# A selective scan on one core: eight scan units in flight instead of four, C products two units at a time, sums three units later in TensorE's order

## The reference, cut to what matters

```python
proj = hidden_states @ W_in.T
u, gate = jnp.split(proj, 2, axis=-1)            # 1024 channels each
u = silu(conv1d(u) + conv_b)                      # 4 taps, depthwise
dt, Bm, Cm = jnp.split(u @ Wx.T, [32, 48], -1)    # each rms-normed, 16 states
delta = softplus(dt @ Wdt.T + dt_bias)
state = exp(delta_t * A) * state + (delta_t * u_t) * B_t     # per step t
y_t = sum over the 16 states of state * C_t
y = (y + u * D_param) * silu(gate)
return y @ W_out.T
```

## Time and profile before

| | |
|---|---|
| runs (3) | 1966.2 to 1977.37 us, median 1969.73 |
| profiled execution | 1971.7 us, span 1969.9 us |
| PE busy | 1608.2 us, 82% |
| DVE busy | 1381.4 us, 70% |
| ACT busy | 1091.1 us, 55% |
| POOL busy | 1009.7 us, 51% |
| mean granted clock of PE | 0.83 of full |

### The profile page before, as it was taken

The page is one execution under the profiler, slowest core; times in us unless marked ns, Lnnn a source line. Parts: engine busy times, 40 slices in busy tenths (PEclk is TensorE's granted clock), DMA queues, the critical chain, the costliest instruction groups (busy, mean ns, idle before and its releaser), DMA issues. The chain is left out here.

```text
span 1969.9 us, 24262 instructions
## 1 busy us (share of the span) xinstructions
PE 1608.2 (82%) x8168; PEld 855.9 (43%) x8168; DVE 1381.4 (70%) x2292; ACT 1091.1 (55%) x2026; POOL 1009.7 (51%) x598
## 2 busy tenths in 40 slices
PE   6888999999779983888597796987978879735768
PEld 2522233222155442665174573655746547402532
DVE  3258888887084115059989888889888898999323
ACT  2333666667621114367767567576675766754127
POOL 0000000001044003449998888989889988999303
PEclk8866999999875995889597796987968879756769
DMA  5311000000094439243544444535344444453122
GB/s 223 152 52 55 3 3 3 3 3 3 12 312 180 130 128 325 81 107 87 122 103 103 107 93 107 125 85 123 92 108 116 98 103 103 108 117 86 38 91 86
DMA packets 152988, 195.78 MB, mean 99 GB/s; under 512 B 17907, under 2 KB 123139, under 8 KB 151198
## 3 DMA queue, kind: packets, MB, share of 16 engines
q1 hardware_dynamic: 143692, 167.19, 32.3%
q0 software_dynamic: 4608, 16.80, 2.3%
q10 hardware_dynamic: 4564, 10.24, 1.4%
HBM read 141.81 MB, written 52.37 MB: 99 GB/s over the span
## 5 line engine op out<-in xcount | busy, mean ns | idle before, releaser
L1808 DVE TENSOR_TENSOR_SCAN ssm_scan<-ssm_psum,ssm_state,ssm_scan 128x256 f32<-128x256 f32 x1024 | 677.6, 728 | 67.8 <-ACT ssm_psum L1695 66.1
L1431 POOL TENSOR_TENSOR ssm_scan<-ssm_scan,ssm_bc 128x1024 f32<-128x1024 f32 x256 | 553.3, 2176 | 52.9 <-DVE ssm_scan L1808 51.8
L1695 ACT ACTIVATE ssm_psum<-ssm_rep,ssm_a 128x256 f32<-128x256 f32 x1024 | 430.9, 468 | 117.4 <-DVE ssm_scan L1808 115.0
L1535 PE MATMUL ssm_psum<-ssm_scan,ssm_select 128*32 128x256 f32 x2048 | 202.3, 476 | 214.5 <-POOL ssm_scan L1431 214.1
L1411 POOL TENSOR_TENSOR ssm_scan<-ssm_rep,ssm_bc 128x1024 f32<-128x1024 f32 x128 | 301.1, 2353 | 63.3 <-PE ssm_psum L1535 51.6
L641 ACT ACTIVATE att_probs<-att_psum 128x1024 f32<-128x1024 f32 x256 | 248.4, 1021 | 106.0 <-PE att_psum L577 105.8
L678 DVE TENSOR_REDUCE att_rowmax<-att_psum 128x1 f32<-128x512 f32 x448 | 277.9, 682 | 39.6 <-PE att_psum L559 39.5
L1535 PEld LDWEIGHTS ssm_psum<-ssm_scan,ssm_select 128*32 128x32 f32 x2048 | 45.7, 119 | 329.4 <-POOL ssm_scan L1431 225.6
L530 POOL COPY att_v<-v_tokens 128x128 f32<-128x128 f32 x8 | 2.3, 291 | 329.5 <-ACT att_out L635 329.5
L559 PE MATMUL att_psum<-att_k,att_q 72*128 72x512 bf16 x448 | 159.8, 397 | 3.7 <-DVE att_rowmax L678 2.2
L1793 DVE TENSOR_TENSOR ssm_scan<-ssm_rep,ssm_psum 128x1024 f32<-128x1024 f32 x128 | 155.5, 1215 | 10.4 <-PE ssm_psum L1535 8.1
(11 more groups left out here) (232 smaller groups left out, 1905.3 us busy)
## 6 DMA issues: line engine op xcount, KB each, us to landing
ssm_rep<-drive_rows SPq DMA_DIRECT2D x256, 256.0 KB, 4.6
qkv_wmod<-in_wmod SPq DMA_DIRECT2D x8, 1536.0 KB, 12.0
late_weights<-in_we SPq DMA_DIRECT2D x8, 1024.0 KB, 14.8
ssm_bc<-bc_rows SPq DMA_DIRECT2D x32, 256.0 KB, 5.0
drive_rows<-ssm_delta SPq DMA_DIRECT2D x64, 128.0 KB
drive_rows<-ssm_du SPq DMA_DIRECT2D x64, 128.0 KB
sorted_rows<-moe_zeros SPq DMA_DIRECT2D x1, 5888.0 KB, 18.9
moe_sorted<-sorted_rows SPq DMA_DIRECT2D x23, 256.0 KB, 3.5
```

The lines of the kernel that those rows point to most:

```text
L1431: nc.gpsimd.tensor_tensor(read[:, Q % RING], drive[:, Q % RING], bc[:, c % 2, 1, gr, :].unsqueeze(1).to_broadcast([P, J, SW]), ALU.mult).t ...
L1535: last = nc.tensor.matmul(ps_y[t % 2][32 * j:32 * j + 32, :], select[:], read[:, Q % RING, j, :], start=(gr == 0), stop=False)
L1695: nc.scalar.activation(ps_decay[n % HALF_BANKS][:, i], rep[:, s % 2, 0, j, :], ACT.Exp, scale=amat[:, t, gr, j:j + 1]).then_inc(decay_done, 1)
L1808: nc.vector.tensor_tensor_scan(drive[:, Q % RING, j, :], ps_decay[(2 * Q + j // 2) % HALF_BANKS][:, j % 2], drive[:, Q % RING, j, :], stat ...
```

## The change

- `RING` is 8. A spread waits for the sum of eight units before; POOL issues its spread three units ahead, at the odd unit.
- The C product is one instruction of 128x2048 for an even unit and the odd one after it, issued when both are scanned.
- PE issues at position q first `misc`, then the sum of unit q - 3 (`LAG`); the last three sums follow the loop.
- `gate_y` goes to the third unit after a tile's end, and writes over `gate`; the tile `y` is gone. So the gate of a chunk can be copied only after the output product of two chunks before.
- The four `out` products take positions 10, 11, 12, 14, where `gate` was, and `gate` takes 16, 17, 27, 28, where `out` was. The copies follow: `OUT_COPY` at 12, 13, 14, 16, `GATE_OUT` at 18, 19, 29, 30, and the gate's silu at 31, after being at 20.
- On SP the store of a chunk's output goes to t = 5 of the next chunk, the load of the residual to t = 1.

```diff
-    RING = 4
+    RING = 8
...
-        y = sb("ssm_y", [P, 2, DT, SW])
...
         AT = {0: ("proj", 0), 1: ("proj", 1), 3: ("conv", 0), 4: ("proj", 2), 5: ("conv", 1), 6: ("proj", 3), 7: ("conv", 2),
-              9: ("conv", 3), 10: ("gate", 0), 11: ("gate", 1), 12: ("gate", 2), 13: ("rows", 0), 14: ("gate", 3), 15: ("square", 0),
-              16: ("out", 0), 17: ("out", 1), 19: ("rms", 0), 21: ("step", 0), 22: ("step", 1),
-              24: ("step", 2), 25: ("step", 3), 27: ("out", 2), 28: ("out", 3)}
+              9: ("conv", 3), 10: ("out", 0), 11: ("out", 1), 12: ("out", 2), 13: ("rows", 0), 14: ("out", 3), 15: ("square", 0),
+              16: ("gate", 0), 17: ("gate", 1), 19: ("rms", 0), 21: ("step", 0), 22: ("step", 1),
+              24: ("step", 2), 25: ("step", 3), 27: ("gate", 2), 28: ("gate", 3)}
...
-        U_COPY, CONV_OUT, GATE_OUT = {3: 0, 4: 1, 7: 2, 9: 3}, {6: 0, 8: 1, 10: 2, 12: 3}, {13: 0, 14: 1, 15: 2, 17: 3}
-        SILU, ROWS_OUT, RMS, GATE_SILU, H_OUT = 13, 16, 18, 20, 24
+        U_COPY, CONV_OUT, GATE_OUT = {3: 0, 4: 1, 7: 2, 9: 3}, {6: 0, 8: 1, 10: 2, 12: 3}, {18: 0, 19: 1, 29: 2, 30: 3}
+        SILU, ROWS_OUT, RMS, GATE_SILU, H_OUT = 13, 16, 18, 31, 24
...
-        OUT_COPY = {19: 0, 20: 1, 30: 2, 31: 3}
-        GATE_Y, DRIVE = 2, 1
+        OUT_COPY = {12: 0, 13: 1, 14: 2, 16: 3}
+        GATE_Y, DRIVE, LAG = 3, 1, 3
...
-                    if t == 1 and c >= 2:
-                        store(c - 2)
+                    if t == 5 and c >= 1:
+                        store(c - 1)
...
-                    if t == 2 and c >= 1:
+                    if t == 1 and c >= 1:
                         load_residual(c - 1)
...
-                    if Q + 2 < SCH * UNITS and not ON_DVE[(q + 2) % UNITS]:
-                        spread(Q + 2)
-                    pool.wait_ge(scan_done, (Q + 1) * J)
-                    nc.gpsimd.tensor_tensor(read[:, Q % RING], drive[:, Q % RING],
-                                            bc[:, c % 2, 1, gr, :].unsqueeze(1).to_broadcast([P, J, SW]), ALU.mult).then_inc(read_done, 1)
+                    if gr % 2:
+                        if Q + 3 < SCH * UNITS:
+                            spread(Q + 3)
+                        pool.wait_ge(scan_done, (Q + 1) * J)
+                        pair = slice((Q - 1) % RING, Q % RING + 1)
+                        nc.gpsimd.tensor_tensor(read[:, pair], drive[:, pair],
+                                                bc[:, c % 2, 1, gr - 1:gr + 1, :].unsqueeze(2).to_broadcast([P, 2, J, SW]), ALU.mult).then_inc(read_done, 2)
...
-                    nc.tensor.matmul(bank("out", c, m)[:, 0:SW], wout[:, t, m * P:(m + 1) * P], y[:, c % 2, t, :], start=(t == 0), stop=False)
+                    nc.tensor.matmul(bank("out", c, m)[:, 0:SW], wout[:, t, m * P:(m + 1) * P], gate[:, c % 2, t, :], start=(t == 0), stop=False)
...
-                    sum_states(c, q)
+                    Q = c * UNITS + q - LAG
+                    if Q >= 0:
+                        sum_states(Q // UNITS, Q % UNITS)
+            for q in range(UNITS - LAG, UNITS):
+                sum_states(SCH - 1, q)
...
-                    act.wait_ge(ygate_done, (c - 1) * DT)
+                    act.wait_ge(out_mm, (c - 1) * KT)
...
-                if c >= 2:
-                    dve.wait_ge(out_mm, (c - 1) * KT)
-                nc.vector.tensor_tensor(y[:, c % 2, t, :], ps_y[t % 2], gate[:, c % 2, t, :], ALU.mult).then_inc(ygate_done, 1)
+                nc.vector.tensor_tensor(gate[:, c % 2, t, :], ps_y[t % 2], gate[:, c % 2, t, :], ALU.mult).then_inc(ygate_done, 1)
```

More of the change, by code:

```diff
@@ L1377, in _ @@
             load_residual(SCH - 1)
-            store(SCH - 2)
             store(SCH - 1)
@@ L1420, in _ @@
             drive_input(0, 1)
-            for Q in range(2):
+            for Q in range(4):
                 if not ON_DVE[Q]:
```

## The result

The changed kernel takes 2074.16 us, the median of four runs (2061.33 to 2081.42), against 1973.55 of the kernel before on the same chip (1966.2 to 1977.9): a ratio of 1.0507, 95% interval 1.044 to 1.0573. It is slower, as forecast, but by 100 us and not by 14; 2074 lies outside the range. The profiled execution is the slowest of the four, 2081.42 us.

The account below looks back on a forecast made before the run. PE was taken to bound units 0 to 18, DVE and ACT the rest. A full chunk of 125.6 against 124.4 us gave +7.2 over six, chunk 0 +2, the last +5.2: +14.4, 1984 us on the median, range 1942 to 2005.

Parts of the forecast that it names:

- the loop's own term: On POOL, du, write, rep, spread and pair product close a circle: 15.7 us a tile, 126 a chunk.
- The full part: First 18 units of a chunk, PE's products back to back: 4.2 us a unit, 16.6 a tile, hiding most of POOL's loop.
- The landing: Four `rep` DMAs in POOL's loop, from issue to the fall of the DMA share: 6.3 us.
- The write: After `du` in POOL's loop, writing to DRAM and waiting for it: 2.2 us.
- the dearer loop: Rival on POOL's loop: rep lands in 7.7 in several tiles, 17 us a tile, 2006 in all; chance 0.06.
- The last chunk: At 118 us it has no cover for six turns of POOL's loop: loss 5.2 us, bounds 0 and 12.
- units 0 to 18: First part of a chunk, PE full: 69.4 us against 69.7 before, so no gain.
- 18 to 26: Units after the first part: gate's silu leaves position 20, saving 1.5 us, so 30.9 against 32.4.
- 26 to the next unit 0: Chunk's end, late gate products and silu at 31: 24.2 us, between 22.9 and 25.3, against 23.9 before.
- Chunk 0: First chunk, without `out`: gets the silu at 31 and loses the wait at 20, +2 us.
- well under half of 208: Sign to look for afterwards: PE's wait for POOL's C product falls well under half of its 208 us.
- the first part gains nothing: Units 0 to 18: decay waits turn into `gate_y` waits for PE; bounds a gain of 3.5 and loss of 2.5 us.

Follow-up runs that it names:

- the first experiment: The changed kernel with `du` issued ahead of the spread and pair product in POOL's pass, nothing else moved: 1984.1 us, ratio 1.0046 to the kernel before.

## Why the prediction was off in size

**The step that failed is the loop's own term:** "Sum 15.7 us a tile, 126 a chunk. The full part runs at 4.2 a unit, 16.6 a tile, and hides it". The loop was found, with all its members in the right order; its length is 16.95. By members, forecast against the changed kernel:

| member | forecast | measured |
|---|---|---|
| `du` | 0.7 | 0.73 |
| write to DRAM and the wait for it | 2.2 | 2.65 mean; 2.2 in 41 of 62 tiles, 2.8 to 4.0 in 21 |
| `rep`, from issue to the spread's start | 6.3 | 7.1 |
| spread | 2.3 | 2.31 |
| pair product | 4.1 | 4.14 |
| sum | 15.7 | 16.9 |

Two terms are short. *The landing* was taken from issue to the fall of the DMA share. The share falls after 6.3 us in the changed kernel too (1141.4 to 1147.7), but POOL starts only 1.0 us after that, at 1148.63. The whole time from issue to a consumer that stands waiting could have been read before the change, at the scan's start, where POOL waits for the first `rep`. SP's issue and POOL's row there, in the kernel before:

```profile
842.97 1.80 SPq L1339 DMA_DIRECT2D ssm_rep<-drive_rows  x4
...
850.04 2.36 POOL L1411 TENSOR_TENSOR ssm_scan<-ssm_rep,ssm_bc 128x1024 f32<-128x1024 f32 x1 [10.55 <-DMA ssm_rep<-drive_rows]
```

850.04 - 842.97 = 7.07. *The write* was taken from one tile. Its 2.2 us is the usual value, in the kernel before too, but in the changed kernel a third of the tiles takes some 1.3 us more, and a loop costs the mean of its turns. That mean couldn't be read before the change: the same stretch had a mean of 2.6 there, but more than half of what it had over 2.2 was SP waiting for ACT's decays to free the `rep` buffer, and SP has no such wait in the changed kernel. What lengthens a third of the writes stays open.

**Why 1.25 us a tile made the 86 us that were missing.** The cover for the loop (the work beside which it runs unseen) was 16.6 us a tile in the full part and 124.4/8 = 15.55 over a chunk. At 15.7 a tile the loop is just above the mean and below the full part; at 16.95 it is above both, so there is no part of a chunk left where it can catch up, and the chunk is eight turns whatever the rest does: 8 x 16.95 = 135.6, measured 135.8. The forecast had this number: the dearer loop was put at "17 us a tile, 136 in the parts of the chunk that don't hide it", and then charged with "+2 a chunk over the forecast", 2006 in all. Against a chunk of 124.4 six chunks of 136 are +70, and +68 is what came. A chance of 0.06 was too low as well: with the text's own upper values, 7.7 for the landing and 4.3 for the pair, the sum is 17.3.

**The direction** was right for the reason given, but it stood on less than the +14 says, and that part is luck. The forecast's chunk of 125.6 us was built against the parts of one chunk, and those add up to 69.7 + 32.4 + 23.9 = 126.0 before; it was compared with 124.4, the mean of the chunks. Like with like, six chunks come out at -2.4 and not at +7.2, and the whole at +5, which its own measure calls no change.

**The last chunk.** Forecast +5.2, or +15 with the dearer loop; measured +21. The forecast gave it six turns from a head start. But POOL comes into it already at the loop's rhythm, so it has eight like the others, 135.8 us, and 142.8 - 135.8 = 7 us for the end. This is read from the sums; no run isolates it.

**What held,** with the loop open in the first experiment: units 0 to 18 took 1177.55 - 1107.36 = 70.2 us (forecast 69.4), 18 to 26 30.5 (30.9), 26 to the next unit 0 25.8 (24.2, 25.3 at PE's lower clock). The waits of `gate_y` at units 7 and 15 are there, the third forecast for unit 11 is not. The silu at 31 makes unit 31 wait 3.2 us, where it had waited 1.0, and moving the silu takes that wait away. Chunk 0 takes 133.6 us against 131.1 (forecast +2). So a forecast made of those parts and of no loop would have been about right: the whole miss is the loop. In the changed kernel itself these parts can't be seen, since the loop stretches all of them, and the sign that PE's wait for the C product would be "well under half of 208" failed there (268.6) for that reason.

**The pages.** The pair product took 4163 ns against the 4497 of the Trainium skill (GPSIMD Engine Reference, "Performance versus the Vector engine"), which was measured there for an add; the row's straight line from 256 and 1024 columns gave 4.1, and this trace goes with the line. The fit that the Trainium skill gives in DMA: Bandwidth & Descriptors ("Anatomy of one DMA"), stated there for one DMA issued by GpSimd, makes an estimate of 4.4 us for a megabyte. Here four DMAs issued by SP took 7.1 to a waiting consumer, so the trace doesn't bear it out for this use, and its error has the sign that would have hidden the loop altogether.

**What the forecast missed besides,** and the runs found: "the first part gains nothing" holds for a lag of three only. A lag of two with single products, loop open, takes 125.2 a chunk to 121.5, and 24 to 36 us in all by the pairs of kernels that differ in just that (1969 to 1945, 1973 to 1937, and by the ratios 1.0046 to 0.9865). In the traces, from the first copy of B to the last `gate_y`, it is 30 to 32 us in all three pairs. The silu at 5 instead of 31 is worth 15 us by the medians of one pair (1.0046 to 0.9969, not run side by side) and 5 by another (1951 to 1945, within their scatter); the same stretch of the traces has 4.6 and 6.3 us (1005.2 to 1000.6, 975.4 to 969.1), most of it in chunk 0. `gate_y`'s wait falls from 67 to 17 us: with sums two units later, the one that it needs is issued a unit earlier in PE's full part. The two edits were not run apart with the loop open. But the kernel with single products and a lag of three, whose loop costs nothing, still has 64.7 us of this wait and (1731.9 - 980.1)/6 = 125.3 us a chunk, which speaks for the lag as the edit that gives it.

## What to carry to other kernels

When an engine's issue order is changed, look at each instruction whose result comes back through another queue, and write down what now stands between it and the instruction that makes the next one. If that closes a circle, sum it from issue to the consumer's start, with the mean of every member and not its usual value, and compare it with the period of the work. Below the period it cost nothing here; above it, nothing hid it, and it was paid in every turn: 2.2 us more in the loop cost 80 us. The sum made here was 7% short; where one comes within 10% of the period, break the circle (here by three lines moved) rather than rely on the margin.

## What was not expected of the hardware

Between the last packet of a `rep` and the start of POOL, which waited for it, lie 0.6 to 1.0 us, 0.8 in the mean of the 25 transfers of the changed kernel that had the queue to themselves. A two-input product of POOL over 2048 columns takes 4163 ns against 2 x 2176 for two of 1024: merging saves 0.19 us a pair. And 1.62 us of memsets behind each `du` didn't make the changed kernel slower.
